# A four-layer attention and feed-forward kernel: the key and value projections move into the first half of the first feed-forward, its second half goes through PSUM, and the plain attentions work on scores in two halves

## The reference

```python
def act_quant_fake(x):
    scale = 127.0 / clip(max(abs(x), axis=-1), 1e-05)
    return clip(round(x * scale), -128.0, 127.0) / scale
def bitlinear(x, w, b):                      # w: signs times one mean
    return act_quant_fake(x) @ weight_quant_fake(w).T + b
h = layernorm(x, ln1_g, ln1_b)               # over 128
h = gelu(bitlinear(h, w1, b1))               # to 512
h = layernorm(h, ln2_g, ln2_b)               # over 512
h = bitlinear(h, w2, b2)                     # to 128, added to x
...
score = q_heads @ k_heads.T * scale          # layer 1 masks keys
out = softmax(score) @ v_heads
x = x + (out @ wo + bo)
```

## Time and profile before

| | |
|---|---|
| median of three runs | 2219.87 us |
| the profiled execution: time, span | 2223.47 us, 2221.7 us |
| mean granted TensorE clock | 0.815 |
| busy: PE, PEld, DVE, ACT, POOL | 1669.8, 1169.6, 1527.2, 761.7, 827.1 us |
| `bit_ffn` with its norm | from about 356 to 604 us |
| plain attentions, first to last subtraction | 631.9 to 774.4, 1079.5 to 1201.5, 1747.8 to 1876.4 us |

### The profile page before, as it was taken

The page is one execution under the profiler, slowest core; times in us unless marked ns, Lnnn a source line. Parts: engine busy times, 40 slices in busy tenths (PEclk is TensorE's granted clock), DMA queues, the critical chain, the costliest instruction groups (busy, mean ns, idle before and its releaser), DMA issues. The chain is left out here.

```text
span 2221.7 us, 46993 instructions
## 1 busy us (share of the span) xinstructions
PE 1669.8 (75%) x14496; PEld 1169.6 (53%) x14499; DVE 1527.2 (69%) x3673; ACT 761.7 (34%) x1619; POOL 827.1 (37%) x866
## 2 busy tenths in 40 slices
PE   3999963336478888997788699928999787359993
PEld 2777752024356664664576344416777566335551
DVE  4999975968678853446787899874655688763332
ACT  1444440346533332332343588700000343122221
POOL 1888841245323216006231000005555232028783
PEclk9999975568779978998798899958999699555555
DMA  3222201026511151111122477516774111424446
GB/s 112 68 66 64 64 21 35 0 68 155 149 44 50 34 163 45 41 39 42 49 55 54 140 306 310 211 22 220 277 274 180 40 56 35 120 49 82 81 82 143
DMA packets 237864, 224.70 MB, mean 101 GB/s; under 512 B 105218, under 2 KB 222787, under 8 KB 230339
## 3 DMA queue, kind: packets, MB, share of 16 engines
q1 hardware_dynamic: 213906, 152.79, 23.2%
q10 hardware_dynamic: 9520, 55.94, 7.1%
q0 software_dynamic: 14336, 14.69, 3.7%
HBM read 127.84 MB, written 92.90 MB: 99 GB/s over the span
## 5 line engine op out<-in xcount | busy, mean ns | idle before, releaser
L627 POOL TENSOR_TENSOR at_KM<-at_K,at_mask 128x512 f32<-128x512 f32 x96 | 99.7, 1039 | 328.2 <-PE at_psS L652 240.9
L702 ACT ACTIVATE at_ET<-at_psT 128x512 f32<-128x512 f32 x192 | 114.6, 597 | 245.4 <-PE at_psT L661 245.4
L1968 POOL TENSOR_TENSOR gr_work<-gr_ring 128x512 f32<-128x512 f32 x96 | 121.6, 1278 | 102.8 <-DVE gr_work L2004 95.7
L737 DVE TENSOR_REDUCE at_mx<-at_psS 128x16 f32<-128x1024 f32 x96 | 117.5, 1224 | 55.7 <-PE at_psS L652 55.4
L2057 PEld LDWEIGHTS gr_psY<-gr_wd,gr_work 128*128 128x128 f32 x1024 | 133.9, 195 | 39.0 <-DVE gr_work L2004 23.0
L2057 PE MATMUL gr_psY<-gr_wd,gr_work 128*128 128x128 f32 x1024 | 141.5, 282 | 10.8 <-DVE gr_work L2004 10.7
L388 POOL TENSOR_TENSOR at_E<-at_Z,at_mx 128x512 f32<-128x512 f32 x128 | 130.8, 1042 | 50.4 <-DVE at_mx L513 50.4
L674 PE MATMUL at_psO<-at_VZ,at_ET 128*64 128x18 f32 x3072 | 110.1, 215 | 40.6 <-ACT at_ET L702 40.5
L661 PE MATMUL at_psT<-kept_ident,at_Z 128*128 128x128 f32 x768 | 131.3, 296 | 10.6 <-DVE at_Z L750 5.1
L674 PEld LDWEIGHTS at_psO<-at_VZ,at_ET 128*64 128x64 f32 x3072 | 101.3, 141 | 58.8 <-ACT at_ET L702 37.3
L1890 PE MATMUL gr_psV<-kept_xT,gr_wu 128*128 (+1 forms) x256 | 125.9, 592 | 0.8 <-ACT gr_V L1759 0.8
(11 more groups left out here) (551 smaller groups left out, 4372.2 us busy)
## 6 DMA issues: line engine op xcount, KB each, us to landing
gr_spill<-gr_ring SPq DMA_DIRECT2D x28, 1792.0 KB, 5.7
gr_ring<-gr_spill ACTq DMA_DIRECT2D x28, 1792.0 KB, 7.2
at_amask<-mask_Bx16xSxS_ff SPq DMA_DIRECT2D x128, 128.0 KB, 2.9
kv_values<-bit_VS SPq DMA_DIRECT2D x32, 432.0 KB, 5.5
at_VZ<-kv_values SPq DMA_DIRECT2D x96, 144.0 KB, 2.2
kv_keys<-bit_KS SPq DMA_DIRECT2D x16, 384.0 KB, 2.7
at_K<-kv_keys SPq DMA_DIRECT2D x96, 64.0 KB, 1.9
cap_acc<-cap_zero SPq DMA_DIRECT2D x2, 2112.0 KB, 12.5
```

The source lines that it names most:

```text
L627: pool.tensor_tensor(KM[:, s % 2, :, :], K[:, s, :].unsqueeze(1).broadcast_to([P, 4, P]), mask4[:, :].unsqueeze(2).broadcast_to([P, 4, P]) ...
L702: act.activation(ET[:, 4 * a:4 * a + 4, :].rearrange("p r q -> p (r q)"), psT[:, :], ACT.Exp, scale=QK_SCALE).then_inc(exped, 1)
L737: dve.tensor_reduce(mx[:, :].rearrange("p (g v) -> p g v", v=4), psS[:, :, 0:256].rearrange("p g (v k) -> p g v k", k=SEQ), AX.X, ALU.max) ...
L1968: pool.tensor_tensor(tp[:, s % 4, :], ring[:, s // 4, first, :], ring[:, s // 4, first + 1, :], ALU.mult).then_inc(pooled, 1)
```

## The change

- In `attention_rows`, scores, maxima and subtractions are made in two halves of two banks each. TensorE's order becomes weigh(i-1), turn(0)(i), project_out(i-2), score(0)(i+1), turn(1)(i), score(1)(i+1), turn_o(i-1), project_q(i+2). VectorE's becomes top(0)(i), measure(i-3), shift(0)(i), top(1)(i), residual(i-2), shift(1)(i), weigh_down(i-1). The first half of the scores waits only for the first subtraction of the tile before. With a mask each half has its own lower limit.
- In `bit_ffn`, the key and value projections and their copies move from the second to the first half, seven jobs a group (three key jobs of 512 columns, four value jobs), through the two banks of `psY`. ScalarE copies four jobs before its transposed copy and three between the gelus. The writes are per group now, keys in rows of 2 KB. `KS` lies in `hn`, so ScalarE waits for all writes before the second half. TensorE's first half is written out in full.
- GpSimd adds b2 to x in the first half. In the second, the limits stand in PSUM (`psH` bank 2), ScalarE scales `hn` into `psH` banks 0 and 1 and adds the rounding constant there, VectorE clips in place in PSUM, and ScalarE makes the integers from PSUM. The residual is one instruction a tile.

```diff
@@ attention_rows: TensorE
-                def score(i, s, n):
+                def score(a):
+                    def half(i, s, n):
...
+                        wait_past(pe, shifted, 2 * i - 1 + a)
...
+                            for g in (2 * a, 2 * a + 1):
+                                chans = slice(32 * g, 32 * g + 32)
+                                last = pe.matmul(psS[rows, g, 0:256], Q[chans, s % 2, rows], KM[chans, s % 2, :, rows],
+                                                 start=keep_mask is None, stop=True)
+                        last.then_inc(scored, 1)
-                run(pe, [(-1, weigh), (0, turn(0)), (-2, project_out), (1, score), (0, turn(1)), (-1, turn_o), (2, project_q)])
+                run(pe, [(-1, weigh), (0, turn(0)), (-2, project_out), (1, score(0)), (0, turn(1)), (1, score(1)), (-1, turn_o), (2, project_q)])
@@ attention_rows: VectorE
+                def top(a):
+                    def half(i, s, n):
+                        mine = mx[:, 8 * a:8 * a + 8]
+                        dve.wait_ge(scored, 2 * i + a + 1)
+                        wait_past(dve, shifted, 2 * i - 1 + a)
+                        dve.tensor_reduce(mine.rearrange("p (g v) -> p g v", v=4), scores(a), AX.X, ALU.max).then_inc(maxed, 1)
+                        if keep_mask is not None:
+                            dve.wait_ge(maxed, STEPS * (2 * i + a) + 1)
+                            dve.tensor_scalar(mine, mine, floor[:, 0:1], None, ALU.max).then_inc(maxed, 1)
...
-                run(dve, [(0, top), (0, shift(0)), (0, shift(1)), (-1, weigh_down), (-3, measure), (-2, residual)])
+                run(dve, [(0, top(0)), (-3, measure), (0, shift(0)), (0, top(1)), (-2, residual), (0, shift(1)), (-1, weigh_down)])
@@ bit_ffn: tiles and SP
-        KS = sb("KS", [P, 2, LAYERS, 2 * P])
-        VS = sb("VS", [P, 2, 2 * LAYERS, 2, VW])
+        KS = hn[:, 0:LAYERS, :, :].rearrange("p l u w -> p u l w")
+        VS = sb("VS", [P, 2, 4 * LAYERS, 2, VW])
...
+        h_int = psH[:, 0:2, :]
+        top2, limit2 = psH[:, 2, 0:2], psH[:, 2, 2:4]
+        JOBS = LAYERS + 4
...
+                def write_kv(g, u, n):
+                    sp.wait_ge(kv_taken, JOBS * (g + 1))
+                    sp.dma_start(keys[:, :, bass.ds(4 * P * g, 4 * P)].rearrange("l p w -> p l w"), KS[:, u, :, :]).then_inc(kv_out[u], 16)
                     for b in range(2):
+                        dst = values[bass.ds(4 * g, 4), :, :, b * VW:b * VW + VW].rearrange("i l (t k) w -> k (i l) t w", t=2)
                         sp.dma_start(dst, VS[64 * b:64 * b + 64, u, :, :, :]).then_inc(kv_out[u], 16)
@@ bit_ffn: VectorE, second half
-                    c.link(dve.tensor_scalar(hn[:, s, 0, :], hn[:, s, 0, :], scale2[:, 0:1], 127.0, ALU.mult, ALU.min))
-                    c.link(dve.tensor_scalar(hn[:, s, 1, :], hn[:, s, 1, :], scale2[:, 1:2], 127.0, ALU.mult, ALU.min))
-                    dve.tensor_scalar(h, h, -128.0, MAGIC, ALU.max, ALU.add).then_inc(rounded, 1)
+                    c.link(dve.tensor_reduce(top2, hn[:, s, :, :], AX.X, ALU.max, apply_absolute_value=True))
+                    c.link(dve.tensor_scalar(limit2, top2, EPS, 1.0 / 127.0, ALU.max, ALU.mult))
+                    dve.tensor_scalar(undo2[:, s, :], limit2, wmean[:, 1:2], None, ALU.mult)
+                    dve.reciprocal(scale2[:, s % 2, :], limit2).then_inc(scale2_ready, 1)
+                def clip_h(k, s, n):
+                    dve.wait_ge(scaled2, k + 1)
+                    dve.tensor_scalar(h_int, h_int, MAGIC + 127.0, MAGIC - 128.0, ALU.min, ALU.max).then_inc(rounded, 1)
...
-                        last = dve.scalar_tensor_tensor(y[:, j, :], psY[:, s % 2, j * D:j * D + D], undo2[:, s, j:j + 1], b2[:, :], ALU.mult, ALU.add)
-                    dve.tensor_tensor(tiles, tiles, y[:, :, :], ALU.add).then_inc(x_added, 1)
+                        last = dve.scalar_tensor_tensor(mine, psY[:, s % 2, j * D:j * D + D], undo2[:, s, j:j + 1], mine, ALU.mult, ALU.add)
...
-                pipelined(dve, PAIRS, [(-2, residual), (0, quantise_h), (-3, measure_x)], period=4)
+                dve.wait_ge(b2_added, G)
+                pipelined(dve, PAIRS, [(0, find_scale_h), (-2, residual), (-3, measure_x), (0, clip_h)], period=4)
@@ bit_ffn: GpSimd, first half
+                    tiles = m.X[:, bass.ds(4 * g, 4), :]
+                    pool.tensor_tensor(tiles, tiles, row(b2), ALU.add).then_inc(b2_added, 1)
@@ bit_ffn: ScalarE
+                def take_kv(g, u, n, q):
+                    act.wait_ge(projected, JOBS * g + q + 1)
+                    if q == 0:
+                        wait_past(act, kv_out[u], 48 * n)
+                    bank = (u + q) % 2
+                    if q < LAYERS:
+                        act.activation(KS[:, u, q, :], psY[:, bank, :], ACT.Identity, bias=kb[:, q:q + 1]).then_inc(kv_taken, 1)
+                        return
...
                         act.activation(H[:, i, :], H[:, i, :], ACT.Gelu).then_inc(gelued, 1)
+                        if j < 3:
+                            take_kv(g, u, n, JOBS - 3 + j)
...
-                pipelined(act, G, [(1, take), (0, gelu)])
+                pipelined(act, G, [(0, take_first), (1, take), (0, gelu)])
...
+                def to_scale_h(k, s, n):
+                    act.wait_ge(scale2_ready, k + 1)
+                    wait_past(act, hq_ready, k)
+                    for j in range(2):
+                        last = act.activation(psH[:, j, :], hn[:, s, j, :], ACT.Identity, bias=plus[:, 0:1], scale=scale2[:, s % 2, j:j + 1])
+                    last.then_inc(scaled2, 1)
...
-                pipelined(act, PAIRS, [(-1, take_h), (2, normalise), (0, to_integers), (0, take_kv)], period=4)
+                for u in range(2):
+                    act.wait_ge(kv_out[u], 48 * G // 2)
+                pipelined(act, PAIRS, [(0, to_scale_h), (-1, take_h), (2, normalise), (0, to_integers)], period=4)
@@ bit_ffn: TensorE
-                pipelined(pe, G, [(0, up), (1, turn)])
+                def project_kv(first, end):
+                    def jobs(g, u, n):
+                        for q in range(first, end):
+                            wait_past(pe, kv_taken, JOBS * g + q - 1)
+                            bank = (u + q) % 2
+                            if q < LAYERS:
+                                pe.matmul(psY[:, bank, :], kw[:, q, :], m.ctxT[:, bass.ds(4 * P * g, 4 * P)], start=True, stop=True).then_inc(projected, 1)
+                            else:
+                                pe.matmul(psY[:, bank, 0:LAYERS * D], m.ctxT[:, bass.ds(P * (4 * g + (q - LAYERS)), P)],
+                                          vw[:, :, :].rearrange("p l d -> p (l d)"), start=True, stop=True).then_inc(projected, 1)
...
+                pipelined(pe, G, [(0, up), (0, project_kv(0, JOBS - 3)), (1, turn), (0, project_kv(JOBS - 3, JOBS))], unrolled=True)
...
-                pipelined(pe, PAIRS, [(-1, down), (0, turn_h), (1, project_kv)], period=4)
+                pe.wait_ge(kv_taken, JOBS * G)
+                pipelined(pe, PAIRS, [(-1, down), (0, turn_h)], period=4)
```

More of the change, by code:

```diff
@@ L115, in plain @@
                     stage(s + lead, (s + lead) % period, (s + lead) // period)
-    if first >= end:
+    if unrolled or first >= end:
         plain(-max(leads), units - min(leads))
@@ L639, in project_q @@
                     pe.matmul(psP[:, 0:P], Wq[:, :], m.xT[:, bass.ds(P * i, P)], start=True, stop=True).then_inc(q_done, 1)
-                def score(i, s, n):
[L642 to L654, removed]
+                def score(a):
+                    def half(i, s, n):
+                        pe.wait_ge(km_ready, i + 1)
+                        pe.wait_ge(q_taken, i + 1)
+                        wait_past(pe, shifted, 2 * i - 1 + a)
+                        if keep_mask is not None:
+                            for g in (2 * a, 2 * a + 1):
+                                pe.matmul(psS[:, g, 0:256], m.identb[:, :], far[:, 0:4, :].rearrange("p v k -> p (v k)"), start=True, stop=False)
+                        for b in range(2):
+                            rows = slice(64 * b, 64 * b + 64)
+                            for g in (2 * a, 2 * a + 1):
+                                chans = slice(32 * g, 32 * g + 32)
+                                last = pe.matmul(psS[rows, g, 0:256], Q[chans, s % 2, rows], KM[chans, s % 2, :, rows],
+                                                 start=keep_mask is None, stop=True)
+                        last.then_inc(scored, 1)
+                    return half
                 def turn(a):
@@ L732, in _ @@
                 STEPS = 2 if keep_mask is not None else 1
[L734 to L741, removed]
+                def top(a):
[4 more added lines that the diff above has]
+                        dve.tensor_reduce(mine.rearrange("p (g v) -> p g v", v=4), scores(a), AX.X, ALU.max).then_inc(maxed, 1)
+                        if keep_mask is not None:
```

(16 more changed lines are left out.)

74 lines of the change are left out of this document (22 added, 52 removed).

## The result

The changed kernel takes 2434.57 us (2432.41 to 2440.56, 4 runs) where the kernel before took 2219.55 beside it: ratio 1.093, 95% interval 1.090 to 1.096. 2204.6 had been forecast. The profiled execution spans 2433.9 us with a mean TensorE clock of 0.745 (before 0.815). Further down, a median and the range beside it are of all executions of a kernel, and a ratio leaves out those more than 1.5% above its fastest one (one of 3852.11 us of the kernel before among them).

A forecast was written before the change was run, and what follows sets the result against it. VectorE bounded the feed-forward's first half; no engine was full in the second, GpSimd waiting for ScalarE. Feed-forward -32.8 us and attentions +17.5 gave -15.3, from 2219.9 to 2204.6 us; range 2174 to 2228.

The forecast's parts named there:

- First half: Feed-forward's first half: DMA writes become the bound and hold the first normalise until 480 us, costing +24 us.
- First normalise at 480, ScalarE released by a DMA: Sign at the start of the feed-forward's second half: ScalarE's first normalise waits for all writes, until 480 us.
- The queue's 80 us for 20.4 MB: Feed-forward's first half: key and value writes need 77 to 82 us, taken as 80, or 10.0 a group.
- Rival 1: Feed-forward's first half: DMA no bound, writes at 318 GB/s, normalise about 470, kernel 2195.5 us; chance 0.13.
- the rule weighed against this term: Feed-forward writes: by the skill, transfers near 1 MB reach 341 GB/s, so 20.4 MB would take 60 us.
- Rival 3: Feed-forward's first half: TensorE stays at half clock, 13.7 us a group, writes end at 506, kernel 2231; chance 0.12.
- Second half: Feed-forward's second half: a two-pair turn gives 5.25 us a pair, 95.5 us in all, next stage at 576.5 for 609.28.
- Rival 4: Feed-forward's second half: scaling into PSUM costs 2.8 us or VectorE still stops, 6.6 us a pair, kernel 2227; chance 0.11.
- The ring: Attentions: residual before shift(1) closes a loop through TensorE and ScalarE, 4.24 us a plain tile against 3.81.
- Rival 2: Attentions: residual finds project_out done, so no loop binds; -16 us for +17.5, kernel 2171; chance 0.14.
- The last leg, turn(1) to weigh: Attentions: from turn(1) to exponent 0.69 us, then exponent and hand-over 0.65, within a 4.24 us plain tile.
- 30 and 27 tiles: Plain attentions: tiles counted at full clock, each +0.43 us, giving +12.9 and +11.6 us.

The follow-up runs named there:

- e9: Changed kernel with 60 bf16 matmuls of zeros (128 x 512) on TensorE ahead of each plain attention's first tile: 2293.36 us.
- e12: Changed kernel with VectorE's order as before, scores still in halves, plus 60 matmuls of zeros ahead of each plain attention: 2334.98 us.
- e10: Changed kernel with the score whole and VectorE's order as before, only the maxima left in halves: 2220.03 us.
- e11: Changed kernel with the score whole, VectorE's order still as changed, plus 60 matmuls of zeros ahead of each plain attention: 2469.67 us.

## Why the prediction was wrong

- **First half, right, with some luck in the number.** "First normalise at 480, ScalarE released by a DMA": 484.3, released by kv_values' write. The queue's 80 us for 20.4 MB are 255 GB/s; it moved 231 to 239 at 0.90 to 0.92 busy between 400 and 480, so it took 87 us (484.3 - 395.4, less the 2 at the ends), outside the 77 to 82 of the prediction. An earlier start hid 2.6 of these 7 us: the first write was issued at 395.4, not 398. Rival 1 (318 GB/s, 470) falls, and with it the rule weighed against this term: the Trainium skill (DMA: Bandwidth & Descriptors, section Measured) has 341 GB/s for 1 MB, measured on loads into SBUF. The trace's writes of 768 and 864 KB, in the other direction, don't come near it, 234. Rival 3 falls too: the clock there was 0.92.
- **Second half, right.** 5.22 us a pair (5.25), scaling into PSUM 0.77 each (1.4 a pair until the next start), clip 1.23 (1.3), end gap 0.96 (1.0). The half takes 95.2 us (95.5). The stage ends 28.9 us earlier for 32.8, the 4 us being the later start. Rival 4 falls.
- **The ring, right in kind, short in one leg.** At full clock a plain tile takes 4.67 us (4.24), and it is for the most part the residual's place that makes it: 0.55 of it goes when only the order goes back. Rival 2 falls: VectorE waits 0.92 us for project_out. Leg by leg from the burst's timeline: weigh to turn(0) 1.05 (1.04), to project_out 0.49, to the residual 0.53 (0.43), to shift(1) 0.20, to turn(1) 0.74. The last leg, turn(1) to weigh, is 1.66 for 1.34 (1149.90 to 1151.56): not the exponent ends it but TensorE itself, with score(1), turn_o and project_q queued ahead of weigh. The prediction let nothing but the exponent end this leg. A half score takes 0.66 us there for the whole one's 0.69 (L652 in the trace before, 16 instructions), so two of them need nearly twice the time of one. By the settled tiles of e9, e12 and e10 (4.65, 4.11, 3.90) the order costs 0.54 and the halves 0.21. In the masked attention the same leg makes a full-clock tile 4.95 us (turn(1) at 704.32 and again at 709.27) for 4.35.
- **The step that failed: the clock of the attentions.** The sum had "30 and 27 tiles" at full clock, from the earlier trace rows and the old cold starts: it took the clock of the old tile order over to the new one without a reason, and only the feed-forward had a rival at half clock. Measured: no plain tile of 64 at full clock. By the burst, the two plain attentions take 289.6 us at full clock and 460.8 without it: **171 us of the loss are the clock**, 39 the tile itself (289.6 - 250.6; in layer 2, with e12 between them, 17.2 for VectorE's order and 5.6 for the halves). With the masked attention's 23 (about 12 of it the tile, 4.95 for 4.57, the rest the clock that came up later), the feed-forward's -29, the 12 between and -3 elsewhere, this is the 212.

The Trainium skill (TensorE: Matmul & The Clock Gate, Part 1) lets the clock follow how busy the array has been of late; by that rule an engine that is busy 99.76 of 100 us would be granted all of it. If busy is what the profile counts so, the trace disagrees: 0.50, for 230 us, twice.

What stays open: what in a tile decides whether the clock comes up. The split score (two empty row groups) and the new order (waits in the ring) each take it away. Bf16 matmuls of full height in each tile give it back; a burst ahead of the stage does so with both edits, not with the new order alone (e11), and with the split score alone (e12) the same code went both ways. The runs show the effects, not the rule. Halves that take some columns of all four groups, so that a half score fills the array, were not tried: the halves would then share the banks of `psS`, which TensorE writes for one half while VectorE reads the other.

## What to carry to other kernels

A gain that is read from a profile at full clock holds only if the new schedule still gets that clock: look at every stage's granted clock in the first profile after a change, before any instruction, and if a busy TensorE stands at half, put cheap bf16 work ahead of the stage or in it as a test; 60 matmuls told here in one kernel that 171 us of the two attentions were the clock. Two other orders did not keep what the same burst gave, so it is a test and no remedy. Splitting work in halves is a gain only where a half costs half: the 32-row matmuls here ran beside each other, so half of their groups took the time of all (0.66 us for 0.69). And when an instruction moves up in one engine's order, follow what it waits for around through the other engines: if it comes back to itself, that sum is the new period.

## What the hardware showed unexpectedly

- Both clock levels can hold themselves with the same instructions: 7.42 us a tile at 0.50 with TensorE 99.8% busy, 4.67 at 1.00 with it 90% busy (125.96 of 140 us, which also hold the ring's waits).
- Adding four bf16 matmuls a tile made the kernel 127 us faster (2434.57 to 2307.45).
- The order of the groups within an unbroken score is free (0.9977 to 1.0040); with another group of instructions (turn(1), 0.66 us) between them, each half takes nearly the time of the whole, 0.66 us for 0.69.
- ScalarE reads 512 columns from SBUF and writes them into PSUM in 0.774 us, 0.762 to 0.783 over 32, beside a GpSimd that is busy 69.14 of 83 us. VectorE's line on the tile in SBUF went from 0.693 to 2.755 us beside GpSimd; the one in PSUM spreads over 1 ns.
